# First graph convolution: source rows picked by a mask product and one maximum, 440 chunks by TensorE, tile sums from paired bf16 one-hots

## The reference, cut to what is touched

```python
h = x @ W                                   # 6250 x 512 by 512 x 8
norm = dinv[src] * dinv[dst]
msg = h[src] * norm[:, None]                # a row of 8 values for each edge
out = jax.ops.segment_sum(msg, dst, num_segments=N) + b
```

## Time and profile before

| | us |
|---|---|
| median of 3 runs (3475.45 to 3489.5) | 3487.32 |
| span of the profiled execution | 3485.4 |
| stage B in it | 190 to 813 |
| its loop of picked groups, first to last matmul | 198.5 to 610.8 |
| its tile sums | 628.3 to 799.3 |

### The profile page before, as it was taken

The page is one execution under the profiler, slowest core; times in us unless marked ns, Lnnn a source line. Parts: engine busy times, 40 slices in busy tenths (PEclk is TensorE's granted clock), DMA queues, the critical chain, the costliest instruction groups (busy, mean ns, idle before and its releaser), DMA issues. The chain is left out here.

```text
span 3485.4 us, 58362 instructions
## 1 busy us (share of the span) xinstructions
PE 2719.8 (78%) x15905; PEld 1951.7 (56%) x15906; DVE 2119.6 (61%) x4040; ACT 1256.3 (36%) x2029; POOL 2093.5 (60%) x2157
## 2 busy tenths in 40 slices
PE   6955557222799999999989995778787878878899
PEld 6945546122577777777777774333343433335687
DVE  8778888986466666666666655333444344443676
ACT  2444457002345444444444554001121212214444
POOL 0067777775777777777760002777777777772454
PEclk9667779556799999999999997999999999998899
DMA  3122233002133333333332324777777777775564
GB/s 100 61 60 48 48 81 80 5 5 54 29 105 98 98 100 94 95 95 103 91 104 94 104 100 157 215 227 232 231 240 232 244 235 246 236 240 170 175 213 128
DMA packets 237234, 459.23 MB, mean 132 GB/s; under 512 B 80060, under 2 KB 102828, under 8 KB 236994
## 3 DMA queue, kind: packets, MB, share of 16 engines
q0 software_dynamic: 111360, 235.84, 25.3%
q1 hardware_dynamic: 125634, 220.46, 19.1%
HBM read 389.41 MB, written 73.25 MB: 133 GB/s over the span
## 5 line engine op out<-in xcount | busy, mean ns | idle before, releaser
L122 POOL DMA_INDIRECT msg_c<-hid_rows,srcT x752 | 762.8, 1014 | 240.1 <-issue 224.9
L1868 POOL DMA_INDIRECT rows<-xn_rows,srcT x784 | 742.9, 948 | 268.6 <-issue 241.6
L2019 PE MATMUL pV<-rows,oh 128*128 x2240 | 554.4, 395 | 143.3 <-DVE oh L2332 59.0
L122 POOL DMA_INDIRECT msg_b<-hid_rows,srcT x464 | 453.5, 977 | 148.3 <-issue 135.8
L1386 PE MATMUL pGc<-xT,wgu_hi 128*128 128x384 f32 (+1 forms) x1848 | 476.7, 380 | 38.7 <-ACT gate_sum L1486 21.7
L2019 PEld LDWEIGHTS pV<-rows,oh 128*128 x2240 | 223.6, 100 | 459.9 <-issue 287.1
L1417 PE MATMUL acc<-wd,hT 128*128 128x512 f32 x1617 | 405.7, 398 | 18.0 <-DVE hT L1630 18.0
L1386 PEld LDWEIGHTS pGc<-xT,wgu_hi 128*128 128x128 f32 x1848 | 340.0, 192 | 105.8 <-issue 60.6
L1417 PEld LDWEIGHTS acc<-wd,hT 128*128 128x128 f32 x1617 | 302.9, 189 | 89.8 <-issue 29.7
L2332 DVE SCALAR_TENSOR_TENSOR oh<-ids,bases,dstT 128x896 f32 x160 | 184.2, 1151 | 225.0 <-issue 161.6
L2320 DVE TENSOR_TENSOR agg<-agg,pV x161 | 110.2, 685 | 321.6 <-PE pV L2019 320.7
(11 more groups left out here) (402 smaller groups left out, 4663.6 us busy)
## 6 DMA issues: line engine op xcount, KB each, us to landing
wd<-wd_rows SPq DMA_DIRECT2D x154, 512.0 KB
we<-in_L_ffn_expert_w SPq DMA_DIRECT2D x16, 1024.0 KB, 8.7
x_rows<-xr SPq DMA_DIRECT2D x49, 256.0 KB, 3.4
xn_rows<-pair SPq DMA_DIRECT2D x49, 256.0 KB, 2.0
rows<-xn_rows,srcT POOLq DMA_INDIRECT x784
res<-x_rows SPq DMA_DIRECT2D x49, 256.0 KB, 3.9
x_rows<-agg SPq DMA_DIRECT2D x49, 256.0 KB, 4.2
xt<-in_x SPq DMA_DIRECT2D x48, 256.0 KB, 2.8
```

What stands on the lines that cost most here:

```text
L122: nc.gpsimd.indirect_dma_start(msg[:, c, :], None, table, bass.IndirectOffsetOnAxis(ap=srcT[:, c:c + 1], axis=0)).then_inc(landed[u % 2], 16)
L1868: nc.gpsimd.indirect_dma_start(rows[:, u % RING, c, :], None, xn2_rows, bass.IndirectOffsetOnAxis(ap=srcT[:, u * Q + c:u * Q + c + 1], axi ...
L2019: last = nc.tensor.matmul(pV[:, ds(to, 1), :].rearrange("p a d -> p (a d)"), oh[:, ds(to, 1), c, :].rearrange("p a d -> p (a d)"), rows[:, ...
```

## The change

Per group TensorE now also gets a mask. SyncE loads the column numbers of the 512 edges too (`hi8`, on 25 partitions, from `hi_rows`, which stage A writes). ScalarE makes their absolute distance from the partition number (`beside`). A matmul with `outside`, a fixed table that holds -2^122 where the columns agree with the partition and 0 elsewhere, adds minus a huge number to every column but the right one. So one maximum over the 25 columns on VectorE, straight from PSUM (`pick`), takes the place of four multiplications and a sum. The second one-hot is made by a comparison on VectorE (`odd`) in place of two activations. `pG` holds three groups (`AHEAD` = 3), which uses the PSUM bank that `ids` had; `lo8` six. TensorE picks `M` = 110 groups (440 chunks), GpSimd gathers 344. The wide pieces come every third group, the down pieces every tenth, and on TensorE and ScalarE one group later than on VectorE. The six steps on `hiT` move behind the loop and work on 32 columns. In the tile sums, destinations are made relative to the tile's first (`rel`, 20 elements), and the one-hots of two chunks are written interleaved from bf16 inputs.

```diff
-M = 80
+M = 110
 MB = 5
+MW = 3
+MD = 10
+AHEAD = 3
 LR = 4
+LB = 6
+OUTSIDE = -2.0 ** 122
 HT = -(-NT // 2)
 assert 4 * M * P <= E and 4 * M % V == 0 and M % MB == 0 and 4 * MB == U
+assert (HT - 1) * -OUTSIDE < 2.0 ** 127
...
-def build(nc, dve, b, c0, t, firsts, dstT, ids, onehot, msg, mstage, ready, msg_ready):
+def build(nc, dve, b, n, c0, t, firsts, dstT, numbers, rel, pairs, msg, mstage, related, ready, msg_ready):
 
     dve.wait_ge(msg_ready, (c0 + (U + VS - 1)) // VS + b * (U // VS))
     at = chunk_at(nc, c0, b, 0, U)
+    nc.vector.tensor_scalar(rel, dstT[:, at], firsts[:, ds(t, 1)], None, ALU.subtract).then_inc(related, 1)
     nc.vector.tensor_copy(mstage[:], msg[:, at, :])
-    nc.vector.scalar_tensor_tensor(onehot[:], bc(ids.unsqueeze(1), (P, U, P)), firsts[:, ds(t, 1)],
-                                   bc(dstT[:, at].unsqueeze(2), (P, U, P)), ALU.add, ALU.is_equal).then_inc(ready, 1)
-
-
-def build_units_beside(nc, dve, t, units_done, free, ended, ranges, firsts, dstT, ids, onehot, msg, mstage, ready, used, msg_ready):
+    dve.wait_ge(related, n + 1)
+    full = (P, U // 2, P, 2)
+    nc.vector.tensor_tensor(pairs, bc(numbers.unsqueeze(1), full), bc(rel.rearrange("p (g j) -> p g j", j=2).unsqueeze(2), full),
+                            ALU.is_equal).then_inc(ready, 1)
...
-            last = nc.tensor.matmul(acc, onehot[:, k, :], mstage[:, k, :], start=False, stop=False)
+            last = nc.tensor.matmul(acc, pairs[:, k // 2, :, k % 2], mstage[:, k, :], start=False, stop=False)
...
+                    own.step(nc.vector.tensor_single_scalar(hi_i[:], src_em[:], 8, ALU.arith_shift_right))
+                    own.step(nc.vector.tensor_copy(high_b[:], hi_i[:]))
+                    dve.sem_inc(s["highs"], 1)
...
-            def piece_at(g):
-                if g < 4 * FB:
-                    return ("wide", g // 2) if g % 2 == 0 else None
-                i, r = divmod(g - (4 * FB + 1), 4)
-                return ("down", i) if r == 0 and 0 <= i < DK else None
+            def piece_at(g, back):
+
+                g -= back
+                if g < 0:
+                    return None, 0
+                if g < MW * 2 * FB:
+                    return ("wide", g // MW) if g % MW == 0 else (None, 0)
+                i, r = divmod(g - (MW * 2 * FB + 1), MD)
+                return ("down", i) if r == 0 and 0 <= i < DK else (None, 0)
...
-                        sp.wait_ge(s["ohs"], g - LR + 1)
-                    sp.dma_start(lo8[:, g % LR, :], lo_rows[g * 4:g * 4 + 4, :].rearrange("c q -> (c q)").partition_broadcast(P)).then_inc(lo_in[g % LR], 16)
+                    if g >= LB:
+                        sp.wait_ge(s["evens"], g - LB + 1)
+                        sp.wait_ge(s["odds"], g - LB + 1)
+                        sp.wait_ge(s["besides"], g - LB + 1)
+                    sp.dma_start(lo8[:, g % LB, :], lo_rows[g * 4:g * 4 + 4, :].rearrange("c q -> (c q)").partition_broadcast(P)).then_inc(lo_in[g % LB], 16)
...
+                nc.gpsimd.affine_select(out=outside[:], in_=outside[:], compare_op=ALU.not_equal, fill=OUTSIDE, base=0,
+                                        pattern=[[0, H], [1, HT]], channel_multiplier=-1).then_inc(s["numbers"], 1)
+                nc.gpsimd.iota(numbers, [[1, P], [0, 2]], base=0, channel_multiplier=0, allow_small_or_imprecise_dtypes=True).then_inc(s["numbers"], 1)
...
-                def select(g):
+                def odd(g):
+                    dve.wait_ge(lo_in[g % LB], (g // LB + 1) * 16)
+                    if g >= AHEAD:
+                        dve.wait_ge(s["prod"], g - AHEAD + 1)
+                    nc.vector.tensor_scalar(los[:, g % AHEAD, 1, :], lo8[:, g % LB, :], lanes[:, 3:4], None, ALU.is_equal).then_inc(s["odds"], 1)
+
+                def pick(g):
                     dve.wait_ge(s["prod"], g + 1)
-                    if g > 0:
-                        dve.wait_ge(s["reduced"], g)
-                    for k in range(4):
-                        last = nc.vector.scalar_tensor_tensor(
-                            masked[:, k], bc(iota[:, 0:HT].unsqueeze(1), (P, H, HT)), hiT[:, 4 * g + k:4 * g + k + 1],
-                            pG[g % 2 * 2 + k // 2][:, k % 2 * H * HT:(k % 2 + 1) * H * HT].rearrange("p (f h) -> p f h", h=HT),
-                            ALU.is_equal, ALU.mult)
-                    last.then_inc(s["masked"], 1)
-                    dve.wait_ge(s["masked"], g + 1)
                     if g >= 2 * MB and g % MB == 0:
                         dve.wait_ge(s["picked"], (g // MB - 1) * 4 - 2)
-                    nc.vector.tensor_reduce(picked[:, g // MB % 2, 4 * (g % MB):4 * (g % MB) + 4, :].rearrange("p c f -> p (c f)"),
-                                            masked[:].rearrange("p c f h -> p (c f) h"), AX, ALU.add).then_inc(s["reduced"], 1)
+                    nc.vector.tensor_reduce(picked[:, g // MB % 2, 4 * (g % MB):4 * (g % MB) + 4, :].rearrange("p (b c) f -> p b (c f)", b=2),
+                                            pG[g % AHEAD][:, :, 0:2 * H * HT].rearrange("p b (c h) -> p b c h", h=HT),
+                                            AX, ALU.max).then_inc(s["reduced"], 1)
...
+                for g in range(AHEAD):
+                    odd(g)
                 for g in range(M):
-                    select(g)
+                    pick(g)
+                    if g + AHEAD < M:
+                        odd(g + AHEAD)
...
-                    act.wait_ge(lo_in[g % LR], (g // LR + 1) * 16)
+                    act.wait_ge(lo_in[g % LB], (g // LB + 1) * 16)
                     if g > 0:
-                        act.wait_ge(s["ohs"], g)
-                    for k in range(2):
-                        last = nc.scalar.activation(far[:, k, :], lo8[:, g % LR, :], ACT.Abs, bias=lanes[:, k:k + 1])
-                    last.then_inc(s["far"], 1)
+                        act.wait_ge(s["evens"], g)
+                    nc.scalar.activation(far[:], lo8[:, g % LB, :], ACT.Abs, bias=lanes[:, 0:1]).then_inc(s["far"], 1)
+                    if g >= AHEAD:
+                        act.wait_ge(s["prod"], g - AHEAD + 1)
+                    act.wait_ge(hi_in[g % LB], (g // LB + 1) * 16)
+                    nc.scalar.activation(beside[:, g % AHEAD, :], hi8[:, g % LB, :], ACT.Abs, bias=lanes[0:HT, 0:1]).then_inc(s["besides"], 1)
                     act.wait_ge(s["far"], g + 1)
-                    if g >= 2:
-                        act.wait_ge(s["prod"], g - 1)
-                    for k in range(2):
-                        last = nc.scalar.activation(los[:, g % 2, k, :], far[:, k, :], ACT.Relu, bias=lanes[:, 2:3], scale=-1.0)
-                    last.then_inc(s["ohs"], 1)
-
-                act.wait_ge(s["lanes"], 2)
-                low(0)
-                low(1)
+                    nc.scalar.activation(los[:, g % AHEAD, 0, :], far[:], ACT.Relu, bias=lanes[:, 2:3], scale=-1.0).then_inc(s["evens"], 1)
+
+                act.wait_ge(s["lanes"], 3)
+                for g in range(AHEAD):
+                    low(g)
                 for g in range(M):
-                    if g + 2 < M:
-                        low(g + 2)
-                    for back in (1, 0):
-                        kind, i = piece_at(g - back) or (None, 0) if g >= back else (None, 0)
+                    for back in (2, 1):
+                        kind, i = piece_at(g, back)
+                        if kind == "down" and back == 2:
+                            down(i, 2)
                         if kind == "down" and back == 1:
-                            down(i, 2)
-                        if kind == "down" and back == 0:
                             down(i, 0)
                             down(i, 1)
-                        if kind == "wide" and back == 0:
+                        if kind == "wide" and back == 1:
                             wide(i)
+                    if g + AHEAD < M:
+                        low(g + AHEAD)
...
-                    pe.wait_ge(s["ohs"], g + 1)
-                    if g >= 2:
-                        pe.wait_ge(s["masked"], g - 1)
+                    pe.wait_ge(s["besides"], g + 1)
+                    pe.wait_ge(s["evens"], g + 1)
+                    pe.wait_ge(s["odds"], g + 1)
+                    if g >= AHEAD:
+                        pe.wait_ge(s["reduced"], g - AHEAD + 1)
                     for k in range(4):
-                        into = pG[g % 2 * 2 + k // 2][:, k % 2 * H * HT:(k % 2 + 1) * H * HT]
+                        into = pG[g % AHEAD][:, k // 2, k % 2 * H * HT:(k % 2 + 1) * H * HT]
+                        nc.tensor.matmul(into, beside[:, g % AHEAD, k * P:(k + 1) * P], outside[:].rearrange("p f h -> p (f h)"), start=True, stop=False)
                         for b in range(2):
                             for j in range(3):
-                                last = nc.tensor.matmul(into, los[:, g % 2, b, k * P:(k + 1) * P], parts[:, j, b].rearrange("p f h -> p (f h)"),
```

(19 more changed lines are left out.)

93 lines of the change are left out of this document (50 added, 43 removed).

## The result

| | kernel before | changed kernel |
|---|---|---|
| median (lowest to highest) | 3488.41 us (3475.45 to 3494.39), 4 runs | 3541.02 us (3534.74 to 3564.09), 4 runs |
| span of the profiled execution | 3485.4 | 3539.7 |
| ratio, 95% interval | | 1.0178 (1.0138 to 1.0218) |
| loop, first to last matmul | 198.5 to 610.8: 412.3 | 182.7 to 703.0: 520.3 |
| from there to the sums' first step | 17.5 | 16.3 |

The change is slower by 1.8%. The forecast was 3429 us, faster by 1.7%. In all but one set of the experiments the chip was one on which TensorE stands still for long while GpSimd gathers and the kernel before takes 5370 to 5424 us, so totals are compared only within a set, and durations are read from stretches without gathers.

What follows compares the result with a forecast made beforehand. It took GpSimd's gathers and VectorE's chain, ending within 17 us of each other, as the bound. Loop end 613.4, sums end 739.7, 59.6 us earlier, less 1.3 for stage A: 3487.3 - 58.3 = 3429 us; range 3385 to 3480.

Steps and rivals of the forecast that it cites:

- 28 matmuls instead of 24 ... 0.086 us each, 2.41 us a group: TensorE in the loop: each group of four chunks takes 28 equally priced matmuls, 2.41 us at full clock.
- No engine needs more than 2.41 us: Loop: with VectorE at 1.45 and ScalarE at 2.05 us a group, 110 groups could pass in 265 us.
- wide cycle: Loop, three groups per wide piece: 3.4 us from transposes to next matmul, 7.2 of matmuls, 1.1 for clock: 11.7 us.
- down cycle: Loop, ten groups per down piece: 34.7 us plus 3.3 for the clock, 38.0 us; three of them counted.
- GpSimd: Gathers beside loop and sums: 344 at 1.31 us end at 644 us, so GpSimd stops being the bound.
- VectorE: Loop: maximum from PSUM 0.95 us, comparison 0.28 (bound 0.69), 1.45 us a group; tile sums: paired comparison 1.49.
- Clock: TensorE in the loop: clock falls in two of three cycles at 1.7 us each, 1.1 us a cycle.
- the range's worst case: Clock falls in every burst as in the first: loop ends 667 us, total 3482; both no-change cases together 0.12.
- Slower: Rival: loop hangs on TensorE at 0.147 us a matmul throughout, ends at 757 us, total 3572; decides from 672; chance 0.06.
- Sums: Tile sums after the loop: 49 tiles at 2.2 us plus 1, 109 us instead of 171, ending at 739.7 us.
- might show: Tile sums: VectorE's queue (branches, range load; 1.93 us at first tile) and TensorE's own (about 1.9 us), hidden under 2.87.
- the rival in which the queues hold the sums: Branches and range load replace the saved comparison: a tile stays 3.1 us, total 3473; both no-change cases together 0.12.

Runs made afterwards that it cites:

- 128-row mask, clean: Changed kernel with the mask matmul on 128 rows and GpSimd's gathers held back until the loop's last group is split; loop 413.9 us, ratio to kernel before 0.965.
- f1_change: The changed kernel as it is, run again on a chip where the kernel before takes 5374.5 us; ratio to the kernel before 0.989.
- g1_order_again: The fast version: changed kernel with 128-row mask and ScalarE's one-hots ahead of the casts, gathers not held back; 3384.45 us, ratio 0.970 to the kernel before.

## Why the prediction was wrong

The step that failed is one term: "28 matmuls instead of 24 ... 0.086 us each, 2.41 us a group". A group takes 3.23 us. The row I took the 0.086 from the earlier trace rows shows 24 matmuls of one shape, and I gave the mask their price because it has the same 200 columns. The shape of the mask, 25 partitions, stood in the diff; no row before showed two row counts in turn, so the term had to be bounded as unknown, and it was not. "No engine needs more than 2.41 us" fell with it, and with that the cycle. Of the 112 us between forecast and measurement the loop holds 103.

How far the rest was right, the loop with the 128-row mask shows, since there the group takes the 2.40 us that I assumed:

| | forecast | change | 128-row mask, clean |
|---|---|---|---|
| group at the full clock | 2.41 | 3.23 | 2.40 |
| wait behind wide transposes | 2.6 | 2.56 | 2.56 |
| wide cycle, mean of 21 | 11.7 | 14.7 | 11.5 |
| down cycle, mean of 3 | 38.0 | 44.1 | 37.6 |
| whole loop | 416.9 | 520.3 | 414 |

- **GpSimd**: gathers end at 628 us (forecast 644), and no sum waits for it. Right.
- **VectorE**: the maximum from PSUM takes 0.99 (0.95), the comparison 0.37 on average (0.28, bound 0.69), the paired one-hots 1.48 (1.49). Right but for the comparison, 0.09 short and without effect, since VectorE had time to spare.
- **Clock**: 1.1 us a cycle was right for the short groups. In the change the clock was lower (0.84), and the range's worst case had the cause wrong: it let the clock fall, not the group grow. "Slower" was there as a rival with TensorE as its engine, its break-even at 0.118 us a matmul. In the change a matmul came to 3.23 / 28 = 0.115 us at the full clock already; over the whole loop it was 0.138 (TensorE's busy time with the picks over their 3080, as the 0.116 before), and the loop ended at 703, past the 672 of that rival. The engine and the point were right, the mechanism, a clock that is low throughout, was not. It had 6%.
- **Sums**: 2.2 us a tile forecast, 125.7 / 49 = 2.57 measured. The two things named as "might show" did: in the groups by line VectorE stands 32.8 us ahead of `rels`, 18.2 behind TensorE and 14.6 behind its own queue, 0.67 a tile. Forecast 109 us, measured 125.7: the term was 17 us short. I had put them beside the comparison; a comparison half as long doesn't cover them. So the rival in which the queues hold the sums was right in part.

The timeline of one tile in the changed kernel:

```profile
762.04 0.17 DVE L1067 TENSOR_REDUCE agg<-pW 128x24 f32 x1
...
763.00 0.23 DVE L189 TENSOR_SCALAR rels<-dstT,firsts 128x20 bf16 x1 [0.79 <-PE pW L219]
763.14 0.28 DVE L190 COPY mstage_b<-msg_b 128x480 bf16 x1
763.34 1.49 DVE L193 TENSOR_TENSOR onehot_b<-numbers_b,rels 128x2560 bf16<-128x2560 bf16 x1
...
765.42 0.23 DVE L189 TENSOR_SCALAR rels<-dstT,firsts 128x20 bf16 x1 [0.50 <-issue]
```

- **Loop start**: 182.7, forecast 196.5. This is no gain of the change: the same kernel began at 197.6 in `f1_change`, and over 20 profiles of all kernels the loop began 4 times at 182 to 183, once at 190 and 15 times at 197.5 to 199.5.
- **The sum of it**: 54 us between the two profiles = 108 in the loop - 16 by its start - 1 before the sums - 45 in the sums + 9 behind them. The last, in code that the change doesn't touch, was not explained; the version with the other order has the same 2695 us there. Against the forecast it is + 103 in the loop, - 14 by its start, - 1 before the sums, + 17 in them, + 9 behind them, and - 1 for stage A, which the forecast had added by itself.

With the mask at its forecast price the change would have come to about 3436 us by the clean loops, against 3429. That the two are so close is in part luck: the early start, which isn't the change's doing, makes up for most of what the sums and the stages behind them took too much. But none of those terms is over 17 us, and the loop's own terms fit. It was one unknown price that turned the sign.

## What to carry to other kernels

A small matmul is not priced by its columns alone. On 25 or 64 partitions between neighbours on 128 it cost 0.104 us at each change, so twice, more than the matmul itself; either pad it to their rows (here for nothing but a taller load and activation that were hidden), or put all small ones together. And once a change makes another engine the bound, what that engine waits for must be ordered anew: the one-hots ahead of the cast were worth 85 us with the 128-row mask, by the waits and by the clock that then stays up.

## What the runs showed of the hardware

- Between matmuls on 128 rows, one on 25 or on 64 rows costs 0.21 us above its own 0.086, half of it on each side, at the full clock, and 0.22 above its own 0.165 at the low one. Its weight load starts 0.18 us after the matmul ahead instead of together with it.
- The granted clock follows the waits of TensorE: with 2.56 us waits every 11 to 15 us it was 0.84 to 0.88 in the loop, with gaps under 1 us in the wide part it stood at 1.00 from 197 to 385 us in the fast version:

```profile
197.00:385.00 188.00, 166.54 (x1829) 157.67 (x1830) 180.10 (x423) 131.83 (x209) 142.58 (x143) 1.00 0.49 123
```

- A gather of GpSimd that starts with VectorE's paired bf16 comparison takes 2.12 us instead of about 1.0.
- On four of the five chips of the experiments TensorE almost stopped while GpSimd gathered. The timeline of PE there, in the changed kernel:

```profile
290.58 0.33 PE L1171 MATMUL pG<-parts,los 128*128 128x200 bf16 x1 [2.48 <-issue]
293.37 0.32 PE L1171 MATMUL pG<-parts,los 128*128 128x200 bf16 x1 [2.46 <-issue]
296.17 0.32 PE L1168 MATMUL pG<-outside,beside 25*128 25x200 bf16 x1 [2.48 <-issue]
```

One matmul every 2.8 us with nothing to wait for, elsewhere a single pause of 90 us, while the gathers kept their 1.25 us. On the chip of `g1_order_again` and in the result's profiles nothing of the kind is seen. What stops the instructions was not found. It turns the sign of this change (1.018 on the one kind, 0.989 on the other), so a verdict on a kernel with long gathers holds only for the kind of chip on which it was taken.
